# Quantised feed-forward of a decoder kernel: the scaling pass of five quantisations goes from VectorE to ScalarE

## The reference, cut to what matters

```python
def act_qdq(x):                      # 16 bits, one scale for the whole tensor
    qmax = 2.0 ** 15 - 1.0
    scale = jnp.maximum(jnp.max(jnp.abs(x)) / qmax, 1e-12)
    return jnp.clip(jnp.round(x / scale), -qmax - 1.0, qmax) * scale
def fixed_qdq_u16(x):
    return jnp.clip(jnp.round(x * 65536.0), 0.0, 65535.0) / 65536.0
x = act_qdq(x)
up = act_qdq(x @ lpbq_dequant(w_up).T)
gate = act_qdq(x @ lpbq_dequant(w_gate).T)
sig = fixed_qdq_u16(jax.nn.sigmoid(gate))
gate = act_qdq(gate * sig)
o = act_qdq(gate * up)
return o @ lpbq_dequant(w_down).T
```

## Times and profile before

| | us |
|---|---|
| three executions | 4165.12, 4166.34, 4168.31 |
| median | 4166.34 |
| the profiled execution | 4203.87 |
| its span on the core | 4200.3 |

### The profile page before, as it was taken

One profiled execution on the slowest core, in us unless ns is written; L12 is line 12 of the kernel. 1 busy time (PEld: TensorE's weight loads), 2 busy tenths in 40 slices (PEclk: granted clock), 3 DMA queues, 4 the chain that ended last, 5 costly groups with the idle time before them and its releaser, 6 DMA issues. The chain is left out here.

```text
span 4200.3 us, 55306 instructions
## 1 busy us (share of the span) xinstructions
PE 3126.8 (74%) x18773; PEld 2247.3 (54%) x18773; DVE 2413.4 (57%) x5103; ACT 1716.0 (41%) x4136; POOL 738.6 (18%) x855
## 2 busy tenths in 40 slices
PE   5999988898768787377677571496496538898787
PEld 4666766676556475244444330444495325555465
DVE  6665666656356334666566669798313674555423
ACT  4666565656332222366466431122232114555211
POOL 0000000000100412444234200000110002333422
PEclk8989999999989799698788785798698769999899
DMA  3101111010000366000000000000394000000366
GB/s 103 36 31 33 41 33 33 23 44 28 25 16 1 143 231 225 4 1 1 25 6 4 23 0 0 3 0 9 148 343 150 0 23 3 2 1 1 125 208 225
DMA packets 96624, 247.13 MB, mean 59 GB/s; under 512 B 15936, under 2 KB 62272, under 8 KB 91360
## 3 DMA queue, kind: packets, MB, share of 16 engines
q1 hardware_dynamic: 87520, 219.82, 15.4%
q0 software_dynamic: 8688, 23.78, 1.5%
q10 hardware_dynamic: 144, 0.07, 0.0%
HBM read 204.47 MB, written 39.15 MB: 58 GB/s over the span
## 5 line engine op out<-in xcount | busy, mean ns | idle before, releaser
L2715 DVE SCALAR_TENSOR_TENSOR L0a_xf<-L0a_xc,L0a_conv,L0a_xf 128x256 f32<-128x256 f32 x432 | 205.5, 544 | 114.9 <-ACT L0a_xf L2589 113.7
L2679 POOL TENSOR_TENSOR L0a_sum_sq<-L0a_sum_sq,L0a_sq 128x512 f32<-128x512 f32 x56 | 85.8, 1532 | 1054.2 <-ACT L0a_sq L2624 1054.2
L1103 POOL TENSOR_TENSOR L3x_p<-L3x_p,L3x_rsum 128x512 f32<-128x512 f32 x128 | 132.9, 1040 | 560.8 <-DVE L3x_rsum L1184 560.8
L2724 DVE TENSOR_TENSOR L0a_ru<-bank,L0a_um 128x512 f32<-128x512 f32 x128 | 88.0, 687 | 204.7 <-PE bank L2487 192.4
L1165 DVE SCALAR_TENSOR_TENSOR L3x_s<-bank,L3x_bias 128x512 f32<-128x512 f32 x128 | 86.6, 681 | 156.7 <-PE bank L949 156.7
L2415 PE MATMUL bank<-x_feat,L0a_wx 128*128 128x256 f32 x576 | 154.7, 419 | 17.0 <-DMA L0a_wx<-in_L0a_wx 13.5
L1103 POOL TENSOR_TENSOR L1x_p<-L1x_p,L1x_rsum 128x512 f32<-128x512 f32 x128 | 132.9, 1040 | 193.6 <-DVE L1x_rsum L1184 193.6
L1756 PE MATMUL bank<-L2a_half,L2a_diag 128*128 128x512 f32 x328 | 144.2, 601 | 28.1 <-ACT L2a_diag L1739 28.1
L1107 POOL TENSOR_TENSOR L1a_p<-L1a_p,L1a_rsum 128x128 f32<-128x128 f32 (+1 forms) x256 | 124.0, 506 | 152.5 <-DVE L1a_rsum L1184 147.8
L2501 PE MATMUL bank<-L0a_ru,L0a_vm 128*128 128x256 f32 x512 | 147.6, 411 | 0.0
L2733 DVE TENSOR_TENSOR L0a_ex<-L0a_ex,L0a_qk 128x768 f32<-128x768 f32 x128 | 124.8, 975 | 39.4 <-ACT L0a_ex L2555 24.4
(11 more groups left out here) (715 smaller groups left out, 8419.9 us busy)
## 6 DMA issues: line engine op xcount, KB each, us to landing
L2f_wt<-in_L2f_w SPq DMA_DIRECT2D x23, 2180.0 KB
L0f_wt<-in_L0f_w SPq DMA_DIRECT2D x39, 898.0 KB
L3f_wt<-in_L3f_w SPq DMA_DIRECT2D x39, 768.0 KB
L0a_wx<-in_L0a_wx SPq DMA_DIRECT2D x72, 256.0 KB, 3.1
L0a_wz<-in_L0a_wz SPq DMA_DIRECT2D x32, 512.0 KB, 4.3
L0f_xs<-rows_by_expert SPq DMA_DIRECT2D x39, 128.5 KB, 3.0
L3f_xs<-rows_by_expert SPq DMA_DIRECT2D x39, 128.5 KB
rows_by_expert<-L0f_zeros SPq DMA_DIRECT2D x4, 1028.0 KB
```

Source lines behind the costliest of these rows:

```text
L1103: last = nc.gpsimd.tensor_tensor(both, both, rsum[r % 2][:, i, :].unsqueeze(2).to_broadcast([P, S, NK]), ALU.mult)
L2715: vec.scalar_tensor_tensor(out=xf[q % 4][:, j, :], in0=xc[q % 3][:, j, i:i + T], scalar=conv[:, 2 * p + j, i:i + 1], in1=xf[q % 4][:, j, : ...
```

## The change

A [128, 1] tile `rounder` is added and filled with ROUND by VectorE at the start of the region. The scaling pass with ROUND of five quantisations (gate, sigmoid, up, mix, out) leaves VectorE and becomes an Identity activation in place on ScalarE, with `rounder` as bias and the inverse scale as scale; the remaining passes are the new function `clip`. The quantisation of x stays as it was. ScalarE gets the order shown; nine semaphores are new.

```diff
+        rounder = sb("rounder", [P, 1])
-        def quantise(ch, vec, a, t, low=True):
+        def quantise(ch, vec, a, t):
             ch.link(vec.tensor_scalar(a, a, t[:, 3:4], ROUND, ALU.mult, ALU.add))
+            clip(ch, vec, a)
+        def clip(ch, vec, a, low=True):
             ch.link(vec.tensor_scalar(a, a, -ROUND, QMAX, ALU.add, ALU.min))
             if low:
                 ch.link(vec.tensor_scalar(a, a, -QMAX - 1.0, None, ALU.max))
...
+                def rounded(a, t, done):
+                    nc.scalar.activation(a, a, ACT.Identity, bias=rounder[:, 0:1], scale=t[:, 3:4]).then_inc(sig(done), 1)
...
+                act.wait_ge(sig("scale_gate"), 1)
+                act.wait_ge(ring.emptied, UNITS)
+                rounded(gate[:, 0, :], s["gate"], "gate_rounded")
                 for m in range(MI):
+                    if m + 1 < MI:
+                        rounded(gate[:, m + 1, :], s["gate"], "gate_rounded")
+                    for i in range(UNITS + m * NBLK, UNITS + (m + 1) * NBLK):
+                        take_unit(i)
                     act.wait_ge(sig("gate_q"), m + 1)
                     if m >= 2:
                         act.wait_ge(sig("weighed"), m - 1)
                     nc.scalar.activation(sg[m % 2], gate[:, m, :], ACT.Sigmoid, scale=s["gate"][:, 1:2]).then_inc(sig("sigmoid"), 1)
-                    for i in range(UNITS + m * NBLK, UNITS + (m + 1) * NBLK):
-                        take_unit(i)
+                    act.wait_ge(sig("sigmoid"), m + 1)
+                    nc.scalar.activation(sg[m % 2], sg[m % 2], ACT.Identity, bias=rounder[:, 0:1], scale=65536.0).then_inc(sig("sigmoid_rounded"), 1)
+                act.wait_ge(sig("scale_up"), 1)
+                act.wait_ge(ring.emptied, 2 * UNITS)
+                rounded(up[:, 0, :], s["up"], "up_rounded")
+                rounded(up[:, 1, :], s["up"], "up_rounded")
+                act.wait_ge(sig("scale_mix"), 1)
+                for m in range(MI):
+                    rounded(gate[:, m, :], s["mix"], "mix_rounded")
+                    if m + 2 < MI:
+                        rounded(up[:, m + 2, :], s["up"], "up_rounded")
+                act.wait_ge(sig("scale_out"), 1)
+                for q in range(N // OUT):
+                    rounded(gate[:, :, q * OUT:(q + 1) * OUT], s["out"], "out_rounded")
...
-                    dve.wait_ge(sig("sigmoid"), m + 1)
+                    dve.wait_ge(sig("sigmoid_rounded"), m + 1)
-                    ch.link(vec.tensor_scalar(a, a, 65536.0, ROUND, ALU.mult, ALU.add))
...
+                vec.memset(rounder[:], ROUND)
...
+                vec.sem_inc(sig("scale_gate"), 1)
-                dve.wait_ge(ring.emptied, UNITS)
-                    quantise(ch, vec, gate[:, m, :], s["gate"])
+                    dve.wait_ge(sig("gate_rounded"), m + 1)
+                    clip(ch, vec, gate[:, m, :])
...
+                vec.sem_inc(sig("scale_up"), 1)
-                dve.wait_ge(ring.emptied, 2 * UNITS)
-                quantise(ch, vec, up[:, 0, :], s["up"])
+                dve.wait_ge(sig("up_rounded"), 1)
+                clip(ch, vec, up[:, 0, :])
                 dve.wait_ge(sig("reduced"), 4)
                 scale_of(ch, vec, s["mix"], factor=s["gate"][:, 0:1])
+                vec.sem_inc(sig("scale_mix"), 1)
...
-                        quantise(ch, vec, up[:, m, :], s["up"])
-                    quantise(ch, vec, gate[:, m, :], s["mix"], low=False)
+                        dve.wait_ge(sig("up_rounded"), m + 1)
+                        clip(ch, vec, up[:, m, :])
+                    dve.wait_ge(sig("mix_rounded"), m + 1)
+                    clip(ch, vec, gate[:, m, :], low=False)
...
+                vec.sem_inc(sig("scale_out"), 1)
...
-                    quantise(ch, vec, gate[:, :, q * OUT:(q + 1) * OUT], s["out"])
+                    dve.wait_ge(sig("out_rounded"), q + 1)
+                    clip(ch, vec, gate[:, :, q * OUT:(q + 1) * OUT])
```

## The result

The changed kernel takes 4149.14 us (median of 5 executions, 4142.10 to 4151.18) against 4166.34 (5 executions, 4159.86 to 4168.31): ratio 0.9957, 95% interval 0.9942 to 0.9971, so 12 to 24 us less. The forecast was 4140.2 in a range of 4134 to 4153, 26.1 us less. The direction holds, and the time lies in the range; the gain is 9 us smaller than forecast.

What follows compares the result with a forecast made beforehand. VectorE was taken to bound the gate and mix phases, TensorE the output phase. 15.9 + 11.5 - 0.7 - 0.1 - 0.5 = 26.1 us less than 4166.34 gives 4140.2; own range 4136 to 4146, with rivals 4134 to 4153.

Steps and rivals of the forecast that it cites:

- Price of the pass: ScalarE's in-place pass: 2.09 us on gate, up and mix, 2.00 on the sigmoid, 1.66 at 128x1536.
- Gate phase: Start gains 4.3 us, four further chunks 10.3 at period 11.05 instead of 13.63, last sigmoid pass 1.3: 15.9 less.
- a bound: Gate phase start: if TensorE's clock stays up, chunk 1's clip could start 2 to 3 us earlier, giving 4137.
- Mix phase: Five chunks gain 2.64 us each at 8.43 instead of 11.07, less 1.65 for two exposed passes: 11.5 less.
- Output phase and end: TensorE's first output group starts 0.7 us later; nine new semaphores cost 0.5 at the region's end.
- Fill of `rounder`: Fill ahead of VectorE's first instruction in the region, costing 0.1 us.
- Region: All terms together in the one region that changes: 26.1 us less.
- A: Rival: TensorE, its clock staying low, bounds the gate loop, which gains nothing; 4153 us, chance 0.08.
- The 2.5 us in A's sum: Gate phase amount subtracted beside the loop's 10.3 in 26.1 - 10.3 - 2.5 = 13.3 us, giving 4153.
- B: Rival: Identity is not in Sigmoid's table, each change on ScalarE costs a 1.28 us load; 4142 us, chance 0.05.
- C: Rival: passes don't overlap, VectorE waits for each one on ScalarE; 26 us more, 4193, chance 0.03.
- the last of the sum: Whole program: the other eleven blocks don't change, so 26.1 us come off the median 4166.34, giving 4140.2.

Runs made afterwards that it cites:

- the halves: Two kernels, each with part of the change on the kernel before: gate and sigmoid passes only, ratio 0.9969; up and mix passes only, ratio 0.9983.
- mix_handed: Changed kernel, but in the mix loop ScalarE starts each pass only when VectorE has come to it; one execution, 4200.90 us.
- mix_only: Kernel before with only the scaling passes of up and mix moved to ScalarE; ratio 0.9983.
- before_named: Kernel before plus the rounder tile, its fill and nine semaphores each raised once, no pass moved; one execution, 4213.52 us.

## Why the prediction was right, and where it was off

- **Price of the pass**: 2.08 us on gate, up and mix (2.09 predicted), 2.00 on the sigmoid, 1.65 at 128x1536 (1.66). Shown by the trace.
- **Gate phase**: predicted 15.9 less, measured 16.7. Period 11.05 as predicted. The 0.8 is the step in which TensorE restarts: I let it restart at the low clock as before; its pause was 2.54 us in place of 4.31, the clock came back sooner (four units in 8.65 us in place of 9.47, then 7.13), and VectorE waited less for the last two units. The prediction had this as a bound, of 2 to 3 us.
- **Mix phase**: 11.5 predicted, 11.6 measured; period 8.43 as predicted; exposed waits 2.22 and 1.99.
- **Output phase and end**: 1.2 lost predicted (0.7 and 0.5), 1.4 measured. **Fill of `rounder`**: 0.1 predicted, 0.01 measured.
- **Region**: 26.1 predicted, 27.0 measured, and 16.7 and 12.4 for the halves.
- **Rivals**: A did not come (four units of TensorE take 7.13 us of a period of 11.05, in place of 9.5 to 9.7, and the mean clock in the phase is 0.85 in place of 0.75). The 2.5 us in A's sum are worked out nowhere. B did not come: there is one table load in the region. That identity is in every set is stated by the Trainium skill, page "ScalarE: Activation LUTs", section "Table sets: the hidden batching unit"; the trace agrees, with one load for 6 sigmoids and 32 Identity calls before, among and behind them. That load took 1.28 us and the sigmoid started 0.01 behind it. C did not come, though the single pass is dearer on ScalarE (2.08 against 1.29 us): it ran beside VectorE's work. mix_handed shows what C would have cost.
- **From region to total**: the step that carries the 9 us is the last of the sum, in which I took the region's gain one for one from the median, as if the other eleven blocks did not change. The cross-attention of layer 2 gave back 2.4 to 2.7 us in both profiles of this kernel; some 6 us are left. Of the later comparisons five hold the region's gain within their intervals: 27.0 in 15 to 32, 16.7 in 8 to 18, 33.0 in 24 to 37, 39.4 in 33 to 47, 0.4 in -3 to 8; mix_only's 12.4 lies at the edge of 2 to 12.2. The ratios themselves give 2 to 5 us less than the region in four of the six, about what such a block gives back, and 1 to 2 more in the other two. The first comparison, 12 to 24, does not hold the 27.0; 24.3 would be its edge. That the rest of that gap is scatter is the likely reading and not shown.
- **Luck in the range**: 4149.14 lies outside the range of the forecast itself, 4136 to 4146. It is in 4134 to 4153 because the upper end was lifted to 4153 for rival A, which did not come. The mechanism and its size in the region are no luck (27.0 against 26.1, and each phase within 0.8); that the total lies in the range is in part. The prediction also calls itself wrong above 4150, which doesn't agree with 4153; the median is 0.9 us under that.

## What to carry to other kernels

Moving an elementwise pass from the engine that bounds a loop to an idle one is worth the pass as often as it is in the loop, even where the idle engine takes 1.6 times as long for it (2.08 against 1.29 us), as long as that engine can run ahead by one chunk and its own sum per chunk stays under the loop's. The price is one exposed pass at each point where a scale or a maximum has to be known first; leave the first chunk where it was, and the price is gone (6 us here, 0.8 of it by TensorE's clock). Judge such a change by the distance between two marks in the profile as well as by the total: the region repeated to 0.1 us in a second profile of each kernel, while 29 executions of one kernel moved by 29. And don't take a gain in one region for a gain of the program: untouched blocks had two forms, 2 us apart.

## What was not expected of the hardware

- The same untouched block took 67.8 to 68.1 or 69.6 to 70.5 us, in kernels of both kinds; in the short form TensorE's clock was back at full earlier. The output phase started at a clock of 0.50 after pauses of TensorE of 92.6 us (before) and 82.4 (after) and at 0.59 after one of 81.0 (mix_only), the last worth 1.0 us against before. In before_named, with nine increments on VectorE at the region's start, the clock was 0.50 in place of 1.00 on the same matrix products, 18 us later.
- Two blocks of the program took some 20 us less in one of 13 profiles (45.8 in place of 58.8 to 65.3 us, 92.7 in place of 111.0 to 117.0) and, by the times alone, likely in the other nine executions beside it too. From 20 to 40 us behind the owner instruction of the first block TensorE is busy for 9.4 to 14.5 us in the twelve long ones and for all 20 in the short one (in the second block 5.9 to 11.2, and all 20); what holds it is not named by the profile.
